# Experts' rows weighted and scattered with addition onto two sums per token while the experts run; the combine loads plain rows, and beta is added early

## The chip, the core and the metric

The kernel runs on one core of a Trainium2 chip. The metric is the device time in microseconds (us) of one launch, the median of several runs; the profile shows one execution.

## The reference

For 6250 tokens of 256 features: a layer norm, a graph sum over 100,000 edges and a second-order attention give a residual `x`. Then comes the part that the change touches, a mixture of 16 experts with the two best taken:

```python
z = layernorm(x)
logits = z @ gate_w + gate_b
vals, idx = top_k(logits, 2);  w = softmax(vals)
h = relu(einsum("bsh,ehf->bsef", z, w1) + b1)
expert_out = einsum("bsef,efh->bseh", h, w2) + b2
y = z + sum(w[..., None] * take(expert_out, idx))
out = x + layernorm(y) * gamma + beta
```

256 features, 512 hidden ones, all float32.

## The kernel before

Tokens are padded to 50 tiles of 128, worked in 10 units of 5 tiles. `acc` holds the residual of all of them in SBUF. After the edges and the attention come three stages.

**The gate**, unit by unit. DVE takes row statistics (`gate_front`, unit u + 1), ACT normalizes the five tiles into one of two buffers `zt5[k]` (`gate_z`, L896), PE turns them and forms logits, DVE takes the two best (`gate_back`), PE ranks them within their experts, and DVE writes the destination rows (`idxz`, L1448). POOL then scatters each of the five tiles twice into `z_dram` with indirect DMAs (`scatter_z`, L719), one for each expert chosen. `gate_z` waits until the scatters of the unit two before have read `zt5[k]`. At the end DVE works out from the counts which expert each of the 116 tiles of 128 slots belongs to and where it lies (L1550 to L1562), SP and ACT write a tile of zeros behind each expert's rows (L574, L915), and DVE works out where each token's two results will lie (L1568 to L1575) and the softmax (L1600 to L1605).

**The experts**, a loop over 116 tiles with four in its body. Each engine runs its own loop:

- PE, for tile t: `hidden(t+1)` (L1956, 8 matmuls, each of two passes), then waits for the slots of tile t+2, turns them (`turn_z(t+2)`, L1946 and L1947), then reads the expert's number and forms the outputs y(t) (L1976).
- ACT: ReLU of the hidden features (L934), then copies the turned slots out of PSUM (L921).
- DVE: adds b2 and writes `yo(t)` (L1592), then `copy_w(t+3)` copies the first weights of a later tile's expert (L1583).
- SP, for tile t: once tile t is turned, `load_z(t+4)` (L583) into one of four buffers `zt`; once `yo(t)` is there, its store to `y_dram` (L599) and `load_b2(t+2)` (L587). Each of these first reads a row or an expert number into a register.

**The combine**, unit by unit: POOL gathers 10 tiles of `y_dram` (L741), ACT normalizes the residual again (L943), DVE adds both weighted rows (L1466), takes statistics (L1021, L1025), ACT normalizes (L953), DVE multiplies by gamma (L1481), adds beta (L1486) and the residual (L1487), and SP stores 640 KB (L614).

Of the kernel before, what the change touches and what calls it, by code (L numbers as in the profile page):

```python
# [20 lines left out]
P = 128  # L21
# [44 lines left out]
R = NP + P  # L66
FT = 116
# [42 lines left out]
def program(nc, x, srcT, dstT, wT, wqkvT, bqkv, wprojT, bproj, temp, gate_w, gate_b, w1, b1T, w2, b2,  # L110
            gamma, beta, out):
    with ExitStack() as ctx:
# [21 lines left out]
        z_dram = nc.dram_tensor("z_dram", [ZR, C], F32).ap()  # L134
        y_dram = nc.dram_tensor("y_dram", [FT * P, C], F32).ap()

# [14 lines left out]
        topv = sb("topv", [P, NT, 2])  # L151
        posT = sb("posT", [P, NT, 2])
        expT = sb("expT", [P, NT, 2])
# [170 lines left out]
        mid = sb("mid", [P, 5120])  # L324
# [8 lines left out]
        zt5 = [mid[:, 2560 + 1280 * k:3840 + 1280 * k].rearrange("p (u c) -> p u c", u=U) for k in range(2)]  # L333
# [13 lines left out]
        zeros = mid[:, 2304:2304 + C]  # L347
# [9 lines left out]
        cmpy = mid[:, 3072:3072 + NT * 2 * X].rearrange("p (t e) -> p t e", e=X)  # L357
        cmpt = mid[0:1, 0:FTL * X].rearrange("p (t e) -> p t e", e=X)
        cmpc = mid[:, 0:X * NT].rearrange("p (e j) -> p e j", e=X)
        tau = mid[0:1, 1920:1920 + FTL]  # L360
        thr = mid[:, 2040:2040 + NT]
        etau = mid[0:1, 2096:2096 + FTL]
        rowI = late[0:1, 512:912][:, 0:FTL].bitcast(I32)
        expI = late[0:1, 512:912][:, FTL:2 * FTL].bitcast(I32)
        stau = late[0:1, 512:912][:, 2 * FTL:3 * FTL]
# [3 lines left out]
        yg = [big[:, 2560 * k:2560 * (k + 1)].rearrange("p (k u c) -> p k u c", k=2, u=U) for k in range(2)]  # L369
        zc = [big[:, 5120 + 1280 * k:6400 + 1280 * k].rearrange("p (u c) -> p u c", u=U) for k in range(2)]  # L370
        fc = [big[:, 7680 + 1280 * k:8960 + 1280 * k].rearrange("p (u c) -> p u c", u=U) for k in range(2)]
        fn = [big[:, a:a + U * C].rearrange("p (u c) -> p u c", u=U) for a in (10240, 12064)]
        gamma_b = big[:, 11520:11776]
        beta_b = big[:, 11776:12032]
        rc = big[:, 12048:12048 + U]
        nc5 = big[:, 12056:12056 + U]
# [49 lines left out]
        s_win = sems("s_win", 14)  # L426
# [4 lines left out]
        s_rg = sems("s_rg", NRB)  # L431
# [43 lines left out]
        s_w = sem("s_w")  # L475
        s_z = sem("s_z")
# [31 lines left out]
        NCONST = 26  # L508
# [9 lines left out]
        def _(sp):  # L518
# [1493 lines left out]
```

## Time and profile before

| | |
|---|---|
| median of 3 runs | 2754.63 us (2744.38 to 2778.39) |
| the profiled execution | 2739.31 us, its span 2737.4 us |
| granted TensorE clock, mean of the profiled span | 0.846 of full speed |
| PE / weight loads / DVE busy | 74% / 49% / 59% of the span |
| ACT / POOL busy | 30% / 47% |
| DMA | 243 MB, 89 GB/s on average |

Busy shares are averages over stages that are bound by different things. A stage has to be read by itself, from the timeline: which instruction waits last there, and for what. An engine's name with a q, as SPq, is its sequencer, and a DMA is listed there at its issue. Times "to landing" run from the issue to the semaphore.

### The profile page before, as it was taken

To read this page: it belongs to the slowest core of one execution; us is meant where nothing else is said; L and a number is where in the kernel's file an instruction comes from. 1 tells how busy PE (TensorE), PEld (TensorE's weight loads), DVE (VectorE), ACT (ScalarE), POOL (GpSimd) and SP (SyncE) were. 2 spreads that over 40 slices of the span, in tenths; PEclk is the share of its full clock that TensorE was granted. 3 is DMA by queue.
4 is the path that set the end of the run, shared out by engine and by line. 5 is a ranking of instruction groups with operands and counts; after the bars stand their busy time and mean duration, and the time that the engine had idled before them with its cause. 6 is when DMAs were issued, how large, how long until landed. Compare 5 with 4: busy or idle time off the path is not lost.

```text
span 2737.4 us, 43467 instructions
## 1 busy us (share of the span) xinstructions
PE 2028.5 (74%) x12138; PEld 1334.9 (49%) x12139; DVE 1622.2 (59%) x4163; ACT 819.7 (30%) x2169; POOL 1294.0 (47%) x1239
## 2 busy tenths in 40 slices
PE   4656766888888887888888888888552999999400
PEld 3434543455444453444444444444552999999300
DVE  6888888888888885444444445444444233233377
ACT  4645631111111111222222222222321444444332
POOL 1263343777777775565655566553454000000375
PEclk9768978999999998998989898988555999999755
DMA  5300010222222222232322222247822333333343
GB/s 168 119 31 27 24 28 28 83 81 81 79 80 81 81 82 64 83 89 81 89 77 83 84 89 86 84 76 65 296 73 98 99 106 106 104 105 108 100 120 119
DMA packets 147105, 243.46 MB, mean 89 GB/s; under 512 B 27874, under 2 KB 104932, under 8 KB 146949
## 3 DMA queue, kind: packets, MB, share of 16 engines
q0 software_dynamic: 55488, 149.11, 20.2%
q1 hardware_dynamic: 88500, 89.91, 10.2%
q10 hardware_dynamic: 2960, 2.55, 0.3%
q8 instruction: 75, 1.23, 0.2%
q14 instruction: 82, 0.66, 0.1%
HBM read 190.08 MB, written 51.38 MB: 88 GB/s over the span
## 4 chain that ended last, share of the span: by engine, by line
PE 36%; another core or an unknown queue 7%; issue 6%; DVE 5%; POOL 3%; DMA 2%; ACT 1%; DVEq 1%; SPq 1%; ACTq 0%; POOLq 0%
PE bank L1956 8%; PE b L1716 7%; PE bqk L1976 7%; PE bank L1833 4%; PE bqk L1844 3%; PE b L1728 2%; POOL big L741 2%; DMA big<-xn_dram,big 2%; POOL big L710 1%; PE bank L1916 1%; DVE big L1466 1%; DVE acc L1259 1%; ACT mid L896 1%; DVE big L1249 1%
## 5 line engine op out<-in xcount | busy, mean ns | idle before, releaser
L710 POOL DMA_INDIRECT big<-xn_dram,big x880 | 916.1, 1041 | 529.4 <-issue 201.4
L1716 PE MATMUL b<-big 128*128 128x256 f32 x1760 | 538.4, 434 | 96.8 <-DVE acc L1259 46.2
L1716 PEld LDWEIGHTS b<-big 128*128 128x128 f32 x1760 | 338.1, 210 | 340.2 <-issue 179.8
L1259 DVE TENSOR_TENSOR acc<-acc,b 128x256 f32 x440 | 183.9, 418 | 366.6 <-remote 195.0
L741 POOL DMA_INDIRECT big<-y_dram,idxz x100 | 112.3, 1123 | 491.6 <-issue 484.0
L1249 DVE TENSOR_SCALAR big<-big 128x128 f32<-128x128 f32 x880 | 300.5, 363 | 7.8 <-DVE big L1299 7.7
L879 ACT ACTIVATE big<-bank 128x512 f32<-128x512 f32 (+1 forms) x208 | 105.4, 576 | 501.9 <-PE bank L1833 276.9
L1956 PEld LDWEIGHTS bank<-late,mid 128*128 128x128 f32 x1872 | 228.6, 193 | 7.6 <-DVE mid L1583 1.7
L1956 PE MATMUL bank<-late,mid 128*128 128x128 f32 x1872 | 229.2, 276 | 1.5 <-DVE mid L1583 1.5
L1976 PE MATMUL bqk<-big,mid 128*128 x928 | 219.5, 379 | 0.0
L1592 DVE TENSOR_TENSOR mid<-bqk,mid 128x256 f32<-128x256 f32 x116 | 49.3, 425 | 246.4 <-PE bqk L1976 246.4
L1976 PEld LDWEIGHTS bqk<-big,mid 128*128 128x128 f32 x928 | 167.3, 190 | 17.9
L719 POOL DMA_INDIRECT z_dram<-mid,idxz x100 | 98.8, 988 | 120.9 <-DVE idxz L1448 91.6
L1766 PE MATMUL bqk<-big,mid 128*128 128x512 f32 (+1 forms) x392 | 144.4, 512 | 5.7 <-ACT mid L839 4.9
L1833 PE MATMUL bank<-big 32*128 32x512 f32 (+1 forms) x832 | 140.9, 672 | 9.7 <-ACT big L879 7.1
L934 ACT ACTIVATE mid<-bank,b1c 128x128 f32<-128x128 f32 x464 | 132.6, 368 | 51.6 <-issue 50.5
L846 ACT ACTIVATE big<-bqk 128x256 f32<-128x256 f32 x49 | 18.8, 384 | 369.9 <-DVE big L1296 354.9
L1279 DVE TENSOR_TENSOR big<-big 128x512 f32<-128x512 f32 x200 | 126.2, 685 | 0.0
L879 ACT ACTIVATE mid<-bank 128x512 f32<-128x512 f32 (+1 forms) x208 | 102.9, 582 | 70.8 <-PE bank L1833 53.1
L1279 DVE TENSOR_TENSOR mid<-big 128x512 f32<-128x512 f32 x192 | 121.4, 686 | 0.0
L1766 PEld LDWEIGHTS bqk<-big,mid 128*128 128x128 f32 x392 | 72.2, 194 | 99.4 <-issue 67.3
L674 POOL DMA_INDIRECT big<-sort_dram,idxg x49 | 54.2, 1106 | 138.4 <-DVEq L1116 109.4
(322 smaller groups left out, 3186.3 us busy)
## 6 DMA issues: line engine op xcount, KB each, us to landing
big<-w SPq DMA_DIRECT2D x8, 2048.0 KB
mid<-z_dram SPq DMA_DIRECT2D x120, 128.0 KB, 2.1
mid<-b SPq DMA_DIRECT2D x118, 128.0 KB, 3.0
y_dram<-mid SPq DMA_DIRECT2D x116, 128.0 KB, 1.7
big<-xn_dram,big POOLq DMA_INDIRECT x880
acc<-x_pad SPq DMA_DIRECT2D x10, 640.0 KB, 6.4
xn_dram<-big SPq DMA_DIRECT2D x10, 640.0 KB
y_out<-big SPq DMA_DIRECT2D x10, 640.0 KB
```

The source lines that it names most:

```text
L710: pool.indirect_dma_start(out=gx[t % EB], out_offset=None, in_=xn_dram, in_offset=bass.IndirectOffsetOnAxis(ap=dstA[:, t:t + 1], axis=0)). ...
L741: pool.indirect_dma_start(out=yg[k][:, m, j, :], out_offset=None, in_=y_dram, in_offset=bass.IndirectOffsetOnAxis(ap=idxz[k][:, j, m:m + 1 ...
L879: act.activation(feat[g % 2][h][:, 0:n], bank[h][:, 0:n], ACT.Square).then_inc(s_feat, 1)
L934: a = act.activation(hT[k % 2][:, c, :], ps_hT[k % 2][:, c * P:(c + 1) * P], ACT.Relu, bias=b1c[:, ds(ex * FC + c, 1)])
L1249: v.tensor_scalar(wd[t % (2 * EB)], iotaP, locA[:, t:t + 1], wA[:, t:t + 1], ALU.is_equal, ALU.mult).then_inc(s_d, 1)
L1259: v.tensor_tensor(mine, mine, ps_pair[p % 2][:, 0:C], ALU.add).then_inc(s_add, 1)
L1279: return v.tensor_tensor(kk[k][:, h], window(kd[k], h * DW, [[0, 16], [1, D]]), window(kd[k], h * DW + 1, [[1, 16], [1, D]]), ALU.mult)
L1716: a = pe.matmul(ps_pair[p % 2][:, 0:C], wd[t % (2 * EB)], gx[t % EB], start=(j == 0), stop=(j == 1))
L1766: a = pe.matmul(bqk[:, lo:hi], xT[s % 2][:, c, :], wqkv[:, c, lo:hi], start=(c == 0), stop=(c == 1))
L1833: pe.matmul(bank[h][:, 0:n], sel[D * h:D * (h + 1), g, :], qT[z % 2][D * h:D * (h + 1), 0:n], start=True, stop=True).then_inc(s_sel, 1)
L1956: a = pe.matmul(ps_hT[k % 2][:, f * P:(f + 1) * P], w1c[k % 2][:, c, f * P:(f + 1) * P], zT[k % 2][:, c, :], start=(c == 0), stop=(c == 1))
L1976: a = pe.matmul(ps_y2[k % 2], hT[k % 2][:, c, :], w2s[:, ds(ex, 1), c, :].rearrange("p o f -> p (o f)"), start=(c == 0), stop=(c == FC - 1))
```

## The change

`y_dram` and the gather from it go. Two sums per token take their place in DRAM, `sum_dram[0]` and `sum_dram[1]`. SP stores the gate's normalized rows into the first and zeros into the second. Rows of `z_dram` become 260 elements wide: behind a slot's 256 features lie its token's number, the first expert's number and the two softmax weights, which the gate now works out (`gate_exp` on ACT, six operations more on DVE). In the experts' loop DVE reads these four out of the slot tile (`meta`, three operations), ACT multiplies `yo` by the slot's weight (`weigh`), and POOL scatters the tile with addition onto `sum_dram[t % 2]`, each after the one two tiles before has landed. The slot buffers `zt` go from four to two, `yo` from two to four; `load_z(t+2)` waits for `meta(t)`. The combine loads both sums plainly (two transfers of 640 KB per unit), adds them, takes statistics, normalizes, multiplies by gamma on POOL and adds the residual, to which POOL has added beta during the experts' loop. The gate's loops and the combine's are written out. Rows that pad the slots are written in one transfer at the gate's end (they were zeros written at the start), and the zeros of `sum_dram[1]` at the start.

```diff
...
-        y_dram = nc.dram_tensor("y_dram", [FT * P, C], F32).ap()
+        z_dram = nc.dram_tensor("z_dram", [ZR, ZW], F32).ap()
+        sum_dram = [nc.dram_tensor(f"sum_dram{k}", [NP + P, C], F32).ap() for k in range(2)]
...
-        zt = [mid[:, 256 * k:256 * (k + 1)] for k in range(4)]
-        b2t = [mid[:, 1024 + 256 * k:1280 + 256 * k] for k in range(2)]
-        yo = [mid[:, 1536 + 256 * k:1792 + 256 * k] for k in range(2)]
-        w1c = [mid[:, 2048 + 1024 * k:3072 + 1024 * k].rearrange("p (c f) -> p c f", c=2) for k in range(2)]
-        hT = [mid[:, 4096 + 512 * k:4608 + 512 * k].rearrange("p (c n) -> p c n", c=FC) for k in range(2)]
+        padrow = mid[:, 2264:2264 + ZW]
+        zt = [mid[:, ZW * k:ZW * (k + 1)] for k in range(2)]
+        b2t = [mid[:, 520 + 256 * k:776 + 256 * k] for k in range(2)]
+        w1c = [mid[:, 1032 + 1024 * k:2056 + 1024 * k].rearrange("p (c f) -> p c f", c=2) for k in range(2)]
+        hT = [mid[:, 3080 + 512 * k:3592 + 512 * k].rearrange("p (c n) -> p c n", c=FC) for k in range(2)]
+        yo = [mid[:, 4104 + 256 * k:4360 + 256 * k] for k in range(4)]
...
-            for a in range(0, 20, U):
-                sp.dma_start(z_dram[X * R + a * P:X * R + (a + U) * P, :].rearrange("(p r) c -> p (r c)", p=P),
-                             zero).then_inc(s_zz, 16)
+            for a in range(0, NT, U):
+                sp.dma_start(sum_dram[1][a * P:(a + U) * P, :].rearrange("(p r) c -> p (r c)", p=P), zero).then_inc(s_zz, 16)
+            for k in range(2):
+                sp.dma_start(sum_dram[k][NP:NP + P, :], zero[:, 0:C]).then_inc(s_zz, 16)
+            sp.dma_start(beta_b[:], beta.partition_broadcast(P)).then_inc(s_gb, 16)
...
+            for u in range(NU):
+                sp.wait_ge(s_z, (u + 1) * U)
+                sp.dma_start(sum_dram[0][u * U * P:(u + 1) * U * P, :].rearrange("(u p) c -> p u c", p=P),
+                             zt5[u % 2][:, :, 0:C]).then_inc(s_zst[u % 2], 16)
+            sp.dma_start(z_dram[X * R:, :].rearrange("(r p) c -> p r c", p=P),
+                         padrow.unsqueeze(1).broadcast_to([P, 20, ZW])).then_inc(s_pz, 16)
...
-            for k in range(4):
+            for k in range(2):
                 load_z(k, k)
-            for k in range(2):
                 load_b2(k, k)
             with sp.Fori(0, FT // 4) as i:
                 for k in range(4):
                     t = 4 * i + k
                     sp.wait_ge(f_zT, t + 1)
-                    load_z(t + 4, k)
+                    sp.wait_ge(f_meta, t + 1)
+                    load_z(t + 2, k % 2)
                     sp.wait_ge(f_yo, t + 3)
-                    sp.dma_start(y_dram[ds(t * P, P), :], yo[k % 2]).then_inc(s_yst[k % 2], 16)
                     load_b2(t + 2, k % 2)
+            for k in range(2):
+                sp.wait_ge(s_ztin[k], 16 * (FT // 2 + 1))
+                sp.wait_ge(s_b2in[k], 16 * (FT // 2 + 1))
             for k in range(4):
-                sp.wait_ge(s_ztin[k], 16 * (FT // 4 + 1))
+                sp.wait_ge(s_ysc[k], 16 * (FT // 4))
+            sp.wait_ge(f_w, FT + 3)
             for k in range(2):
-                sp.wait_ge(s_yst[k], 16 * (FT // 2))
-                sp.wait_ge(s_b2in[k], 16 * (FT // 2 + 1))
...
+            for u in range(NU):
+                for k, a in ((0, zc[u]), (1, z1[u])):
+                    sp.dma_start(a, sum_dram[k][u * U * P:(u + 1) * U * P, :].rearrange("(u p) c -> p u c", p=P)).then_inc(s_zl[u // 2], 16)
+                if u == 0:
+                    sp.dma_start(gamma_b, gamma.partition_broadcast(P)).then_inc(s_gb, 16)
+            for u in range(NU):
+                sp.wait_ge(s_fo, u + 1)
+                sp.dma_start(out[u * U * P:(u + 1) * U * P, :].rearrange("(u p) c -> p u c", p=P), zc[u]).then_inc(s_ost, 16)
+            sp.wait_ge(s_ost, 16 * NU)
...
+            for t in range(FT):
+                pool.wait_ge(f_ys, t + 1)
+                if t >= 2:
+                    pool.wait_ge(s_ysc[(t - 2) % 4], 16 * ((t - 2) // 4 + 1))
+                pool.indirect_dma_start(out=sum_dram[t % 2], in_=yo[t % 4], in_offset=None,
+                                        out_offset=bass.IndirectOffsetOnAxis(ap=idxy[t % 4][:, 0:1], axis=0),
+                                        compute_op=ALU.add).then_inc(s_ysc[t % 4], 16)
+                if 4 <= t < 4 + NT:
+                    mine = acc[:, t - 4, :]
+                    pool.tensor_tensor(mine, mine, beta_b[:], ALU.add).then_inc(s_xb, 1)
+            pool.wait_ge(s_gb, 32)
+            for u in range(NU):
+                pool.wait_ge(s_fn, u + 1)
+                pool.tensor_tensor(zc[u], zc[u], gamma_b.unsqueeze(1).broadcast_to([P, U, C]), ALU.mult).then_inc(s_gm, 1)
...
+            def gate_exp(u):
+                act.wait_ge(s_df, u + 1)
+                act.activation(ew[:], df[:], ACT.Exp).then_inc(s_ew, 1)
...
+            for u in range(NU):
+                gate_root(u)
+                gate_z(u)
+                if u:
+                    gate_exp(u - 1)
+                gate_turn(u)
+            gate_exp(NU - 1)
...
+            def weigh(t, k):
+                act.wait_ge(f_yo, t + 3)
+                act.wait_ge(f_meta, t + 1)
+                act.activation(yo[k], yo[k], ACT.Copy, scale=wslot[k][:]).then_inc(f_ys, 1)
...
+            for t in range(1, 4):
+                expert(t, t)
+                weigh(t - 1, t - 1)
...
+                v.wait_ge(s_ew, u + 1)
+                link(v.tensor_scalar(wsum[:], ew[:], 1.0, None, ALU.add))
+                link(v.reciprocal(wsum[:], wsum[:]))
+                link(v.tensor_tensor(wlow[:], ew[:], wsum[:], ALU.mult))
+                mark(v.tensor_tensor(zt5[k][:, :, C + 2], wsum[:], wlow[:], ALU.subtract))
+                mark(v.tensor_copy(zt5[k][:, :, C + 3], wlow[:]))
...
+            def combine_front(u):
+
+                v.wait_ge(s_zl[u // 2], 64)
+                link(v.tensor_tensor(zc[u], zc[u], z1[u], ALU.add))
+                row_stats(lambda j: zc[u][:, j, :], mv[:, u * U:(u + 1) * U, :])
+                v.sem_inc(s_cst, 1)
+
+            def combine_out(u):
+
+                v.wait_ge(s_gm, u + 1)
+                v.tensor_tensor(zc[u], zc[u], acc[:, u * U:(u + 1) * U, :], ALU.add).then_inc(s_fo, 1)
...
+            def meta(t, k, i):
+
+                v.wait_ge(s_ztin[k % 2], 32 * i + 16 * (k // 2 + 1))
+                if not (isinstance(i, int) and i == 0):
+                    v.wait_ge(s_ysc[k], 16 * i)
+                mark(v.tensor_copy(idxy[k][:], zt[k % 2][:, C:C + 1]))
+                link(v.scalar_tensor_tensor(out=wmask[:], in0=zt[k % 2][:, C + 1:C + 2], scalar=etau[:, ds(t, 1)],
+                                            in1=zt[k % 2][:, C + 2:C + 3], op0=ALU.is_equal, op1=ALU.mult))
+                link(v.tensor_tensor(wslot[k][:], wmask[:], zt[k % 2][:, C + 3:C + 4], ALU.add))
+                v.sem_inc(f_meta, 1)
+
             def expert_four(i, first):
                 for k in range(4):
                     t = 4 * i + k
+                    meta(t, k, i)
                     v.wait_ge(f_y, t + 1)
                     v.wait_ge(s_b2in[k % 2], 32 * i + 16 * (k // 2 + 1))
-                    if not (first and k < 2):
-                        v.wait_ge(s_yst[k % 2], 32 * i + 16 * (k // 2))
-                    v.tensor_tensor(yo[k % 2], ps_y2[k % 2], b2t[k % 2], ALU.add).then_inc(f_yo, 1)
+                    v.tensor_tensor(yo[k], ps_y2[k % 2], b2t[k % 2], ALU.add).then_inc(f_yo, 1)
                     copy_w(t + 3, k + 1)
...
-                    pe.wait_ge(s_ztin[(k + 2) % 4], 16 * (i + 1 + (k + 2) // 4))
+                    pe.wait_ge(s_ztin[k % 2], 32 * i + 16 * (k // 2 + 2))
                     turn_z(t + 2, k + 2)
...
```

Beside this the windows of the edge sort and the record gather share semaphores in pairs.

## Rows read from the trace of the kernel before

**Rows 1.** The page: busy tenths of 40 slices, PE and the granted clock.

```profile
PE   4656766888888887888888888888552999999400
...
PEclk9768978999999998998989898988555999999755
```

**Rows 2.** Timeline (start us, us, engine, line): the first and last outputs.

```profile
2128.97 1.89 PE L1976 MATMUL bqk<-big,mid 128*128 x8
...
2558.11 1.89 PE L1976 MATMUL bqk<-big,mid 128*128 x8
```

**Rows 3.** Timeline of one tile of the experts' loop.

```profile
2300.62 1.89 PE L1976 MATMUL bqk<-big,mid 128*128 x8
...
2302.71 0.42 DVE L1592 TENSOR_TENSOR mid<-bqk,mid 128x256 f32<-128x256 f32 x1 [2.27 <-PE bqk L1976]
2303.31 0.35 SPq L599 DMA_DIRECT2D y_dram<-mid  x1
2303.64 0.69 DVE L1583 COPY mid<-big 128x1024 f32 x1 [0.50 <-issue]
...
2304.13 0.27 PE L1946 MATMUL b<-ident,mid 128*128 128x128 f32 x1
...
2304.35 1.89 PE L1976 MATMUL bqk<-big,mid 128*128 x8
2304.55 0.34 SPq L587 DMA_DIRECT2D mid<-b  x1
...
2305.87 0.35 SPq L583 DMA_DIRECT2D mid<-z_dram  x1
```

**Rows 4.** DMA issues: KB each, median us from issue to landing.

```profile
mid<-z_dram SPq DMA_DIRECT2D x120, 128.0 KB, 2.1
...
z_dram<-mid SPq DMA_DIRECT2D x4, 640.0 KB, 12.4
```

**Rows 5.** Timeline of the loop's start: the first slot loads and what they release.

```profile
2118.55 3.69 SPq L583 DMA_DIRECT2D mid<-z_dram  x4
...
2120.74 0.44 PE L1946 MATMUL b<-ident,mid 128*128 128x128 f32 x1 [25.20 <-DMA mid<-z_dram]
...
2122.83 1.28 ACT L926 ACT_TABLE_LOAD   x1
```

**Rows 6.** Timeline of the gate: a unit's last scatter and small operations of DVE.

```profile
2009.86 0.17 DVE L1448 CAST idxz<-posf 128x10 int32<-128x10 f32 x1 [0.32 <-DVE posf L1444]
...
2010.85 0.96 POOL L719 DMA_INDIRECT z_dram<-mid,idxz  x1 [11.87 <-DVE idxz L1448]
...
2022.23 0.96 POOL L719 DMA_INDIRECT z_dram<-mid,idxz  x1 [0.30 <-issue]
...
2024.02 0.24 DVE L1443 TENSOR_TENSOR late<-late 128x80 f32<-128x80 f32 x1
...
2024.86 0.60 ACT L896 ACTIVATE mid<-acc,nbias,rstd 128x256 f32 x1 [1.94 <-DMA z_dram<-mid,idxz]
```

**Rows 7.** Windows: PE, PEld, DVE, ACT, POOL busy us, PEclk, DMA share, GB/s.

```profile
1940.00:1945.00 5.00, 3.89 (x16) 3.10 (x16) 0.97 (x6) 1.20 (x2) 3.78 (x5) 0.50 1.07 377
2564.00:2565.00 1.00, 0.00 (x0) 0.00 (x0) 0.00 (x0) 1.00 (x3) 0.00 (x0) 1.00 0.12 28
2565.00:2566.00 1.00, 0.00 (x0) 0.00 (x0) 0.00 (x0) 1.00 (x3) 0.00 (x0) 0.53 0.04 12
```

**Rows 8.** Groups by line from 2560 us on: busy us, mean ns, idle before.

```profile
L741 POOL DMA_INDIRECT big<-y_dram,idxz x100 | 112.3, 1123 | 491.6 <-issue 484.0 <-DVE idxz L1471 7.7
...
L953 ACT ACTIVATE big<-big 128x256 f32<-128x256 f32 x50 | 25.7, 588 | 18.9 <-DVEq L1477 10.9 <-issue 8.0
...
L1021 DVE BATCH_NORM_STATS2 st<-big 128x6 f32<-128x256 f32 x50 | 17.3, 412 | 0.1
L1487 DVE TENSOR_TENSOR big<-big,acc 128x1280 f32<-128x1280 f32 x10 | 14.9, 1492 | 0.8 <-DVE big L1486 0.3
```

**Rows 9.** One line's instructions: the same POOL operation on 128x1280, ns min/median/max.

```profile
L682 POOL TENSOR_TENSOR acc<-acc,big x10: 2875/3067/4120, 127.9 to 156.0; 128x1280 f32<-128x1280 f32 x10
```

More of the change, by code:

```diff
@@ L66 @@
 R = NP + P
+ZW = C + 4
 FT = 116
@@ L721, in scatter_z @@
                                                 ).then_inc(s_zsc[k][j], 16)
-            pool.wait_ge(s_zz, 16 * 4)
-            with pool.Fori(0, NU // 2 - 1) as i:
-                for k in range(2):
-                    scatter_z(2 * i + k, k)
-            scatter_z(NU - 2, 0)
+            for u in range(NU - 1):
+                scatter_z(u, u % 2)
             pool.wait_ge(s_idxz, NU)
-            pool.memset(zeros, 0.0).then_inc(s_dz, 1)
+            pool.memset(padrow, 0.0).then_inc(s_dz, 1)
@@ L735, in _ @@
[L735 to L743 removed]
+            pool.wait_ge(s_gb, 16)
@@ L940, in combine_z, with combine_root, combine_rows @@
-            def combine_z(u, k):
+                    expert(t, k)
+                    weigh(t - 1, (k - 1) % 4)
+            weigh(FT - 1, (FT - 1) % 4)
+            def combine_root(u):
+                act.wait_ge(s_cst, u + 1)
+                act.activation(std5[:], mv[:, u * U:(u + 1) * U, 1:2].rearrange("p u o -> p (u o)"), ACT.Sqrt, bias=eps[:]
+                               ).then_inc(s_crt, 1)
+            def combine_rows(u):
+                act.wait_ge(s_csc, u + 1)
                 for j in range(U):
@@ L972, in _ @@
+                a.then_inc(s_fn, 1)
+            for u in range(NU):
+                combine_root(u)
+                combine_rows(u)
         @block.vector
@@ L1536, in _ @@
             gate_front(0)
-            unit_scales(0, NU + NK)
-            gate_pair(0, True)
-            loop(1, NU // 2 - 1, gate_pair)
-            gate_pair(NU // 2 - 1, False)
+            scales(0, s_grt, s_gsc)
+            for u in range(NU):
+                if u < NU - 1:
+                    gate_front(u + 1)
+                gate_back(u)
             join()
@@ L1609, in _ @@
             loop(1, FT // 4, expert_four)
-            for k in range(2):
-                v.tensor_copy(idxz[k][:], posT[:, k * U:(k + 1) * U, :]).then_inc(s_idxc, 1)
-            v.sem_inc(s_ask, 1)
-            v.wait_ge(s_gb, 32)
-            combine_front(0, 0, 0)
-            combine_scales(0)
-            combine_pair(0, True)
-            loop(1, NU // 2 - 2, combine_pair)
-            combine_pair(NU // 2 - 2, False)
-            combine_pair(NU // 2 - 1, False, last=True)
+            v.wait_ge(s_xb, NT)
+            for u in range(NU + 2):
+                if u < NU:
+                    combine_front(u)
+                if u >= 2:
+                    combine_out(u - 2)
+                if u < NU:
+                    scales(u, s_crt, s_csc)
         @block.tensor
@@ L1933, in _ @@
             logits(0, 0)
-            with pe.Fori(0, NU // 2 - 1) as i:
-                for k in range(2):
-                    rank(2 * i + k)
-                    logits(2 * i + k + 1, 1 - k)
-            rank(NU - 2)
-            logits(NU - 1, 1)
-            rank(NU - 1)
+            for u in range(NU):
+                rank(u)
+                if u < NU - 1:
+                    logits(u + 1, (u + 1) % 2)
             pe.wait_ge(s_cc, NU + 1)
```

326 lines of the change are left out of this document (126 added, 200 removed).

## The prediction

> **What bounds the kernel now.** I read the page's slices first [rows 1]. PE is 80 to 90% busy through the edges and the attention, drops to 5, 5, 2 tenths in the gate, stands at 9 in the experts' loop and at 0 in the combine. The change leaves the first 1900 us alone but for some zero writes, so three stages count: gate, experts, combine. Next the timeline of each.
>
> The experts' loop is bound by PE. Its outputs y(t) start every (2558.11 − 2128.97) / 115 = 3.73 us [rows 2], and one tile's rows show PE going from y to hidden to turn to the next y with no gap, while DVE waits 2.27 us for PE [rows 3]. 116 × 3.73 = 433 us. Every transfer has slack there: slots are loaded four tiles ahead.
>
> The gate's ends are the scatters: ten in a row, one every (2022.23 − 2010.85) / 9 = 1.26 us, and POOL idle between units, 11.87 us at most [rows 6]. The combine begins where the last y ends, 2558.11 + 1.89 = 2560.0, and takes 2737.4 − 2560.0 = 177.4 us. POOL is busy for 112.3 us of it with 100 gathers [rows 8], and with the 0.3 us of issue beside each they set the pace.
>
> **The experts' loop after the change.** This is where I expect the loss. Two things are new around `load_z`: there are two slot buffers, so tile t+2 goes into the one of tile t, and the load waits for `meta(t)`, since meta reads the last four columns of that buffer. Now put meta into DVE's order: yo(t−1), `copy_w(t+2)`, `meta(t)`. And the load into PE's order: y(t−1), hidden(t+1), **wait for slots t+2**, turn, y(t). So each y(t) needs a load that can't be issued before y(t−1) has ended and DVE has worked off three things. The loop becomes a ring through four engines, and its period is the sum around it:
>
> - y end to the end of yo: 2300.62 + 1.89 = 2302.51 to 2303.13, 0.62 us [rows 3].
> - to the end of the weight copy: 2304.33, another 1.20 us, 0.50 of it reading the expert's number into a register [rows 3].
> - meta: three operations on one column, 0.17 us each by the smallest shown [rows 6], and waits against register values around them. Below: 3 × 0.17 with small gaps, 0.6 us. Above: each gap as long as the 0.50 us of the same engine in the loop [rows 3], 1.5 us. I take 0.9.
> - SP reads the row number and issues: four such loads take 3.69 us, of which the last one's issue is 0.34 as in a load_b2; (3.69 − 0.34) / 3 − 0.34 = 0.78 us of preparation [rows 3, 5], and 0.18 us from yo's end to the store waiting on it shows the signal [rows 3]. 0.9 us; bounds 0.7 and 1.2 (the 0.98 us between L587's end and L583, and the signal) [rows 3].
> - issue to PE: 2120.74 − 2118.55 = 2.19 us [rows 5]; the median landing is 2.1 [rows 4]. Bounds 1.9 and 2.6, the latter for the scatters now running beside it.
> - turn to the start of y: 4.35 − 4.13 = 0.22 us [rows 3]. PE's sequencer then reads the expert's number. Before, it ran ahead of the array; now it has just been stopped, and the read shows. By DVE's 0.50 us for the same read, less the turning beside it: 0.3, bounds 0 and 0.5 [rows 3].
> - y itself: 1.89 us [rows 3].
>
> Sum 0.62 + 1.20 + 0.90 + 0.90 + 2.19 + 0.22 + 0.30 + 1.89 = 8.22 us. hidden (under 2 us) lies inside the wait, so PE stands idle for some 4 us per tile. The granted clock holds for about that long: after the last y at 2560.0 it was 1.00 until 2565 and 0.53 in the microsecond after [rows 7], so it may fall in some gaps. A turning matmul of the loop's cold start took 0.44 us against 0.27 [rows 3, 5], and a y at half clock 1.9 us more. I take a quarter of that, 0.5 us per tile: 8.72. The loop takes 116 × 8.72 = 1012 us, **+579**.
>
> The Trainium skill ("Trainium Kernel Development and Optimization", Best Practices) says to double-buffer so that transfers and compute overlap. It speaks for the change: two buffers would be enough and the loop would stay at 3.73 us. What speaks against it here are the rows: the buffer is given back so late in the ring that both buffers' lead is used up before the load starts.
>
> What else is new in the loop lies beside this. weigh is one more ACT operation of the size of L896, 0.60 us at most [rows 6], per tile, on an engine that would be busy for a quarter of the period. The scatter is issued by POOL in 0.96 us [rows 6]; each waits for the one two tiles before, and the meta of tile t for the scatter of t−4. No row prices a scatter that adds. From below it is the plain scatter, 2.63 us from issue to the next user (2022.23 to 2024.86) [rows 6]; it would have to take over 14 us, nearly two periods, to be felt. The nearest row is the plain one, so I take nothing. Had the loop kept 3.73 us, 6 us would be the limit. Beta on POOL, 50 times a fifth of a 128x1280 operation, 0.6 us each [rows 9], is hidden by POOL's waits, as is the lost y store. By the skill ("DMA: Bandwidth & Descriptors", Anatomy of one DMA) a transfer by POOL costs 2.0 us plus bytes over 436 GB/s, an estimate of 2.3 us for 131 KB; it prices no addition, and the sum is the same.
>
> **The gate.** ACT's order is now root(u+1), z(u+1), exp(u), and z(u+1) waits for the scatters of unit u−1. DVE needs exp(u) before `idxz(u)`, so scatter(u) starts only when scatter(u−1) has landed. From a unit's first scatter: 11.38 to its last, 2.63 to z, 0.60 for z, 1.28 for a table load [rows 5, 6] and some 0.25 for the exp, then DVE's five small operations and the ranks' six, 2.8 us at 0.17 to 0.24 each with gaps, and 1.0 from idxz to POOL (2009.86 to 2010.85) [rows 6]: 19.9 us per unit. Now it is about 18: L719 fills 12.6 and POOL waits for the rest. +2 us on eight units, less what writing out the loops saves: +10, bounds 0 and +20. The end of the gate loses DVE's three large operations and gains one write of 2560 rows (2.7 MB); four transfers that write 640 KB each to the same tensor land 12.4 us after their issue [rows 4], which is about as long as the zero tiles behind the experts take beside it. I take nothing; it is in the +20. The zeros for `sum_dram[1]`, 6.5 MB at the start, run before the first sorted chunk is stored.
>
> **The combine.** The gathers go. From the last y: yo 0.62, weigh about 1.0, the scatter 0.96 + 2.63 [rows 3, 6], then loads of 13.1 MB. In the gate the weights arrive at 377 GB/s [rows 7]; at that rate a unit's 1.3 MB take 3.5 us, and DVE needs more: two adds of 1.49, statistics 17.3 / 10 = 1.73, and 1.3 for the rest, 6.0 us [rows 8]. So DVE is the bound: 5.2 + 2.2 + 7 with the signals about 15 to the first sum, since a pair of units shares its wait; 60 for ten units; and behind the last ACT 25.7 / 10 = 2.6 and a root 0.3, POOL's gamma 3.07 [rows 8, 9], an add 1.49, and a store that I take at 4, twice a slot load [rows 4], with the signals 13: 88 us in place of 177.4, **−89**. Bounds −105 and −65, the last if loads pace it.
>
> **Sum.** Against the profiled execution's 2739.3 us: + 579 + 10 − 89 = 3239 us. The median of the runs lies 15 us above that execution, which I leave inside the range. Forecast **3240**.
>
> **Rivals.**
> - *The load stays hidden.* If two buffers are enough, the loop stays near 3.73 us, and the combine's gain shows: 2739 + 10 − 89 = 2660, faster. It decides below a period of 3.73 + 79 / 116 = 4.4 us. The ring's two certain parts alone, a load of 2.19 and y of 1.89, give 4.1, and DVE's yo and copy 1.8 more, so only a misread order could bring it. 7 in 100.
> - *The clock stays at half.* y takes 1.9 us more and the turning 0.3 in every tile: period 10.4, 2739 + 10 + 774 − 89 = 3434. For it speaks a gap of 4 us per tile; against it that y and hidden, 1.9 us each at full clock, would follow each other for over 7 us at half clock with no gap, and that the loop's start, as cold [rows 5], was followed by 3.73 us per tile throughout [rows 2, 3]. 11 in 100.
> - *The addition is slow.* A scatter-add of 24 us gives a period of 12: 2739 + 10 + 959 − 89 = 3619. Only the lack of a row speaks for it. 4 in 100.
> - *The ring as forecast*, period 7.2 to 9.6: 78 in 100.
>
> **How the numbers follow.** The ring from its low ends is 0.62 + 1.2 + 0.6 + 0.7 + 1.9 + 0.22 + 0 + 1.89 = 7.1, with 7.2 for a little clock: 2739 + 0 + 403 − 105 = 3037. The upper end takes in the half-clock rival: 2739 + 10 + 774 − 80 = 3443. So 3035 to 3445. Slower by over 2% (about what a measurement can tell) in all cases but the first: 0.92. Faster 0.06. Within 2%, 0.02, a period between 4.0 and 4.9, which nothing points to.
>
> **What would show it.** In the profile after, y's starts 8 to 9 us apart; PE waiting for the slot load (L583's successor) in each tile, before the turn; SP issuing that load right behind DVE's meta; DVE idle for y as before; POOL idle for most of the loop. The granted clock in the loop below 1.00 if the 0.5 us is right. The combine some 90 us with DVE busy throughout, and unit starts in the gate 20 us apart. Wrong if PE waits for the scatter or the loop's period is under 5 us.

## The result and the profile after

The changed kernel takes 3382.9 us (median of four runs, 3377.6 to 3402.15), the kernel before 2762.4 us over its four runs (2744.38 to 2778.39). The ratio is 1.226, 95% interval 1.218 to 1.234: slower by 22.6%, some 620 us. The forecast was 3240 us, with a range of 3035 to 3445.

| stage, in the profiled executions | before | after | difference | forecast |
|---|---|---|---|---|
| to the gate's first scatter | 1933.2 | 1975.2 | +42.0 | 0 |
| gate, first to last scatter | 177.3 | 203.9 | +26.6 | +10 |
| last scatter to first y | 18.5 | 20.4 | +1.9 | 0 |
| experts, first y to last matmul of y | 430.6 | 1100.4 | +669.8 | +579 |
| from there to the end | 177.8 | 100.5 | −77.3 | −89 |
| span | 2737.4 | 3400.4 | +663.0 | +500 |

The first row can't be laid to the change. Nearly all code up to there is the same but for the zero writes and the shared semaphores, and the edge gathers begin at 471.2 and 470.2 us. The profiled execution of the kernel before was quicker than all four of its runs (2739 us, median 2762), that of the changed kernel the longest of its own (3402, median 3383). In the study's other profiles the first scatter starts between 1945.0 and 1973.4 us, at 1961.6 in the one whose code there is that of before (before_two_slots); 1933.2 and 1975.2 are the two ends of all twelve. Without this row 621 us are left, as the medians differ.

The page of the changed kernel, busy tenths and granted clock, to be held against [rows 1]:

```profile
PE   5477678888887788878878844366666666666650
...
PEclk8788789999998888889888855587888777777875
```

PE stands at 6 in the experts' loop where it stood at 9, and the clock mostly at 7 and 8 where it was 9. The same shows in a window of the loop (PE, PEld, DVE, ACT, POOL busy, PEclk, DMA share, GB/s):

```profile
2300.00:2500.00 200.00, 128.60 (x546) 105.71 (x546) 31.25 (x105) 40.38 (x126) 48.60 (x42) 0.78 0.22 41
```

One tile of the loop in the timeline, beside [rows 3]:

```profile
2502.21 3.44 PE L1976 MATMUL bqk<-big,mid 128*128 x8 [0.67 <-issue]
...
2505.68 0.42 DVE L1599 TENSOR_TENSOR mid<-bqk,mid 128x256 f32<-128x256 f32 x1 [7.79 <-PE bqk L1976]
2506.61 0.69 DVE L1580 COPY mid<-big 128x1024 f32 x1 [0.50 <-issue]
2506.94 0.34 SPq L612 DMA_DIRECT2D mid<-b  x1
...
2507.52 0.16 DVE L1590 TENSOR_TENSOR wslot<-wmask,mid 128x1 f32<-128x1 f32 x1
2508.62 0.34 SPq L608 DMA_DIRECT2D mid<-z_dram  x1
...
2510.76 0.44 PE L1946 MATMUL b<-ident,mid 128*128 128x128 f32 x2 [3.33 <-DMA mid<-z_dram]
...
2511.73 3.54 PE L1976 MATMUL bqk<-big,mid 128*128 x8 [0.53 <-issue]
```

The ring, the closed chain of waits from one y to the next, is there. y ends at 2505.65; yo, the weight copy and meta follow on DVE to 2507.68; SP issues the slot load at 2508.62; PE, idle for 3.33 us before it turns the slots, names that load as what it waited for, and starts the next y at 2511.73. Grouped by line over the loop (busy us, mean ns, idle before and what ended it):

```profile
L1976 PE MATMUL bqk<-big,mid 128*128 x839 | 355.0, 597 | 49.8 <-issue 49.8
...
L1946 PE MATMUL b<-ident,mid 128*128 128x128 f32 x208 | 54.8, 353 | 309.1 <-DMA mid<-z_dram 309.1
```

The first of these rows in the kernel before:

```profile
L1976 PE MATMUL bqk<-big,mid 128*128 x856 | 202.5, 379 | 0.0
```

Each pass of y lasts 597 ns on average where it lasted 379, and 309 us of PE's idle time end with the slot load, 309.1 / 104 = 2.97 us per tile. Where the clock stood is told by windows over the parts of the tile shown: y, hidden, the wait, the turn with the register read, the next y.

```profile
2502.21:2505.65 3.44, 3.44 (x10) 2.85 (x11) 0.00 (x0) 1.29 (x5) 2.31 (x2) 0.57 0.29 33
2505.65:2507.43 1.78, 1.78 (x16) 1.59 (x15) 1.25 (x4) 0.00 (x0) 0.00 (x0) 1.00 0.08 10
2507.43:2510.76 3.33, 0.01 (x1) 0.01 (x1) 0.22 (x2) 0.00 (x0) 0.00 (x0) 1.00 0.28 79
2510.76:2511.73 0.97, 0.44 (x3) 0.21 (x3) 0.00 (x0) 0.50 (x2) 0.00 (x0) 1.00 0.00 0
2511.73:2515.27 3.54, 3.54 (x9) 2.85 (x10) 0.00 (x0) 1.42 (x5) 2.31 (x2) 0.54 0.28 31
```

The granted clock is full (2.4 GHz) in hidden, through the whole wait and in the turn, and at half (1.2 GHz) for nearly all of both y. In the gate, the units' scatters start 19.3 us apart (2034.03, 2053.33), but for the first distance, 39.5 us, and the last, 17.5:

```profile
2007.40 2.57 ACT L932 ACTIVATE mid<-acc,nbias,rstd 128x256 f32<-128x256 f32 x5 [29.25 <-DMA sum_dram<-mid]
...
2014.74 0.97 POOL L744 DMA_INDIRECT z_dram<-mid,idxz  x1 [27.00 <-DVE idxz L1501]
...
2034.03 0.97 POOL L744 DMA_INDIRECT z_dram<-mid,idxz  x1 [6.85 <-DVE idxz L1501]
...
2053.33 0.97 POOL L744 DMA_INDIRECT z_dram<-mid,idxz  x1 [6.86 <-DVE idxz L1501]
```

ACT waited 29.25 us for the store of an earlier unit into `sum_dram[0]`, which SP had queued behind 16.8 MB of weights: the loads go out from 1952.75 us on, the first store at 1993.74.

### The profile page after: what moved, and what is told of

Its sections match the earlier page's. It is cut to its first block, busy times and chain, and to the rows that moved or that the text cites. A ratio compares the mean times of both kernels' runs of the same rounds, so it can differ in the third digit from the quotient of the medians.

```text
span 3400.4 us, 43794 instructions
## 1 busy us (share of the span) xinstructions
PE 2308.4 (68%) x12138; PEld 1518.1 (45%) x12139; DVE 1622.8 (48%) x4451; ACT 862.5 (25%) x2260; POOL 1440.9 (42%) x1317
## 4 chain that ended last, share of the span: by engine, by line
PE 29%; DMA 9%; issue 9%; another core or an unknown queue 7%; DVE 6%; SPq 4%; DVEq 3%; POOL 3%; ACT 1%; POOLq 0%; ACTq 0%
PE bqk L1976 12%; DMA mid<-z_dram 7%; PE b L1718 6%; PE bank L1835 3%; PE bqk L1846 2%; PE b L1730 2%; PE b L1946 2%; POOL z_dram L744 2%; SPq L607 2%; DVEq L1577 2%; DMA big<-xn_dram,big 1%; SPq L586 1%; POOL big L735 1%; PE bqk L1882 1%
## 5 line engine op out<-in xcount | busy, mean ns | idle before, releaser
L735 POOL DMA_INDIRECT big<-xn_dram,big x880 | 926.6, 1053 | 559.9 <-PE b L1718 237.3
L765 POOL DMA_INDIRECT sum_dram<-mid,idxy x116 | 180.3, 1554 | 905.3 <-ACT mid L967 905.3
L1976 PE MATMUL bqk<-big,mid 128*128 x928 | 392.0, 596 | 56.0 <-issue 56.0
L1976 PEld LDWEIGHTS bqk<-big,mid 128*128 128x128 f32 x928 | 265.3, 299 | 143.9 <-issue 89.9
L1946 PE MATMUL b<-ident,mid 128*128 128x128 f32 x236 | 62.1, 353 | 372.3 <-DMA mid<-z_dram 372.3
L1956 PEld LDWEIGHTS bank<-late,mid 128*128 128x128 f32 x1872 | 291.6, 236 | 16.6
L1956 PE MATMUL bank<-late,mid 128*128 128x128 f32 x1872 | 279.3, 313 | 0.0
L962 ACT ACTIVATE late<-b 128x256 f32<-128x256 f32 x118 | 45.3, 384 | 901.9 <-PE b L1946 901.9
L1946 PEld LDWEIGHTS b<-ident,mid 128*128 128x128 f32 x236 | 27.0, 160 | 394.8 <-DMA mid<-z_dram 367.9
```

The source lines that it names most:

```text
L735: pool.indirect_dma_start(out=gx[t % EB], out_offset=None, in_=xn_dram, in_offset=bass.IndirectOffsetOnAxis(ap=dstA[:, t:t + 1], axis=0)). ...
L765: pool.indirect_dma_start(out=sum_dram[t % 2], in_=yo[t % 4], in_offset=None, out_offset=bass.IndirectOffsetOnAxis(ap=idxy[t % 4][:, 0:1], ...
L1946: a = pe.transpose(ps_zT[k % 2][:, P * c:P * (c + 1)], zt[k % 2][:, P * c:P * (c + 1)], ident[:])
L1956: a = pe.matmul(ps_hT[k % 2][:, f * P:(f + 1) * P], w1c[k % 2][:, c, f * P:(f + 1) * P], zT[k % 2][:, c, :], start=(c == 0), stop=(c == 1))
L1976: a = pe.matmul(ps_y2[k % 2], hT[k % 2][:, c, :], w2s[:, ds(ex, 1), c, :].rearrange("p o f -> p (o f)"), start=(c == 0), stop=(c == FC - 1))
```

## The experiments

All of them start from the changed kernel unless said otherwise. Starts and stage lengths are read as in the table above. A period is the loop's length divided by its 116 tiles; from start to start of y it is up to 0.1 us more (9.55 us in the changed kernel, whose period is 9.49). Where a mean over 111 tiles is given, it is taken from the starts and ends of the instructions in the trace, without the loop's ends.

### Four slot buffers

```diff
...
-        zt = [mid[:, ZW * k:ZW * (k + 1)] for k in range(2)]
+        zt = [mid[:, ZW * k:ZW * (k + 1)] for k in range(4)]
...
-                    load_z(t + 2, k % 2)
+                    load_z(t + 4, k)
...
```

To make room, two of the four `yo` lie in tensors that are free by then (`upper` and `ones`; `mv`, `rstd`, `nbias` and scratch). The waits on the slot loads follow the four buffers.

> The changed kernel with four slot buffers instead of two, load_z(t+4) instead of load_z(t+2); everything else kept (four yo, the wait for meta, the scatter with addition). Theory, the ring through one load: the load has three tiles more of lead, PE no longer waits for it, y starts every 3.7 to 3.8 us again (9.6 now), the loop takes about 435 us in place of 1101, so about 3383 - 666 = 2717 us, range 2690 to 2760: the gain of the combine minus the gate's loss shows. Rival, the scatter with addition sets the pace once the loop is fast: a period of 5 us or more, with POOL or DVE's meta waiting for a scatter, 2860 us or more. Rival, the wait for meta costs even with four buffers: period 5 to 6, PE waiting for the slot load.

Measured: 2718.2 us, ratio to the kernel before 0.984 (0.977 to 0.992). The loop takes 430.7 us, y starts every 3.73 us, the gate 203.8 and the end 100.4 us as in the changed kernel.

```profile
2401.13 1.89 PE L1978 MATMUL bqk<-big,mid 128*128 x8
...
2402.38 1.55 POOL L767 DMA_INDIRECT sum_dram<-mid,idxy  x1 [2.00 <-ACT mid L969]
2402.39 0.34 SPq L608 DMA_DIRECT2D mid<-z_dram  x1
...
2404.86 1.89 PE L1978 MATMUL bqk<-big,mid 128*128 x8
```

```profile
2300.00:2500.00 200.00, 200.00 (x1393) 188.86 (x1393) 91.10 (x269) 102.97 (x323) 106.40 (x80) 1.00 0.59 106
```

The whole loss is in the lead of one load, that is, in how long before its use it is issued. With four buffers PE is busy for all of the 200 us of the window, so the wait for meta costs nothing, and the clock is 1.00. The scatter with addition sets no pace either: POOL waited for an earlier one to land 12 times in 116 (25.4 us in all), and no other engine waited for a scatter.

### The kernel before with two slot buffers

```diff
-                    load_z(t + 4, k)
+                    load_z(t + 2, k % 2)
```

> The kernel before with one thing of the change: two slot buffers, load_z(t+2). There is no meta; the load waits only for the turned tile and for its place in SP's queue, behind the wait for yo(t-1), its store and load_b2. Theory: two buffers alone make a ring. yo 0.62, signal and store 0.53, load_b2 with its preparation 1.24, preparation of the load 0.98, landing 2.19, the turn and the register read 0.97 as in the changed kernel, y 1.89 to 3.5: 8.4 to 10 us per tile, 3300 to 3490 us in all. Rival, only the wait for meta does the harm and two buffers are enough without it: period 3.73, 2762 us as before.

Measured: 3505.5 us, ratio 1.272 (1.261 to 1.283); period 10.1 us, both just above what was expected. So the two buffers do the harm by themselves. Without meta the load still stands in SP's queue behind the wait for yo, its store and load_b2:

```profile
2510.79 0.42 DVE L1592 TENSOR_TENSOR mid<-bqk,mid 128x256 f32<-128x256 f32 x1 [8.48 <-PE bqk L1976]
2511.42 0.36 SPq L599 DMA_DIRECT2D y_dram<-mid  x1
...
2512.77 0.35 SPq L587 DMA_DIRECT2D mid<-b  x1
2514.46 0.34 SPq L583 DMA_DIRECT2D mid<-z_dram  x1
...
2516.49 0.48 PE L1946 MATMUL b<-ident,mid 128*128 128x128 f32 x1 [3.33 <-DMA mid<-z_dram]
...
2517.59 3.78 PE L1976 MATMUL bqk<-big,mid 128*128 x8 [0.41 <-issue]
```

The load is issued 3.25 us behind the end of yo (2511.21 to 2514.46), later than in the changed kernel (2506.10 to 2508.62, 2.52 us), where no store stands before it. The means over 111 tiles are 2.76 and 2.59 us, and y lasts 3.64 us against 3.39.

### Shortening the ring: meta ahead of the weight copy

```diff
...
-                    meta(t, k, i)
+                    if first and k == 0:
+                        meta(t, k, i)
...
                     v.tensor_tensor(yo[k], ps_y2[k % 2], b2t[k % 2], ALU.add).then_inc(f_yo, 1)
+                    if k < 3:
+                        meta(t + 1, k + 1, i)
+                    elif not last:
+                        meta(t + 1, 0, i + 1)
                     copy_w(t + 3, k + 1)
...
```

> The changed kernel, two slot buffers, with DVE's meta(t+1) moved ahead of copy_w(t+3). Theory: the weight copy's 0.50 + 0.69 = 1.2 us leave the ring, the period goes from 9.6 to about 8.4, about 3383 - 140 = 3243 us; a shorter gap of PE may also keep the clock up and give more, down to 3150. Rival, the load doesn't wait for DVE but for SP's own queue: then at most 0.5 us per tile, 3325 us or more.

Measured: 3364.4 us, 18.5 less than the changed kernel; period 9.26 where 9.49 was. The theory's number was wrong and the rival's right:

```profile
2508.43 0.42 DVE L1600 TENSOR_TENSOR mid<-bqk,mid 128x256 f32<-128x256 f32 x1 [6.38 <-PE bqk L1982]
...
2509.08 0.16 DVE L1590 TENSOR_TENSOR wslot<-wmask,mid 128x1 f32<-128x1 f32 x1
2509.72 0.34 SPq L612 DMA_DIRECT2D mid<-b  x1
...
2511.09 0.34 SPq L608 DMA_DIRECT2D mid<-z_dram  x1
...
2513.21 0.69 PE L1952 MATMUL b<-ident,mid 128*128 128x128 f32 x2 [2.59 <-DMA mid<-z_dram]
```

Meta now ends at 2509.24, but SP had turned to load_b2 first, and the slot load follows it by 1.37 us. From yo's end (2508.85) to the load it is 2.24 us, 0.28 less than before the edit (2.26 and 2.59 us in the means). 0.28 × 116 = 32 us by the ring; 26 us of the loop's length were measured.

### The same, with the slot load ahead of load_b2

```diff
...
                     load_z(t + 2, k % 2)
-                    sp.wait_ge(f_yo, t + 3)
-                    load_b2(t + 2, k % 2)
+                    sp.wait_ge(f_yo, t + 2)
+                    load_b2(t + 1, (k + 1) % 2)
...
```

> meta_first (3364 us) with SP's order turned: load_z(t+2) goes out before load_b2, which is moved a tile back. Theory, in meta_first the slot load stood behind load_b2 in SP's queue (issued 1.37 us behind it), which ate the 1.2 us gained on DVE: now the load is issued some 0.7 us earlier, period 9.26 to 8.5, about 3364 - 80 = 3284 us, range 3220 to 3310. Rival, SP's order doesn't matter: 3364 us.

Measured: 3147.4 us, 217 less than meta_first where 80 were expected. The direction was right, the size not: in the tile shown the load goes out 1.59 us behind yo's end, 0.65 us earlier, and the period fell by 1.89 us (7.37).

```profile
2500.92 1.99 PE L1983 MATMUL bqk<-big,mid 128*128 x8 [0.53 <-issue]
...
2502.95 0.42 DVE L1601 TENSOR_TENSOR mid<-bqk,mid 128x256 f32<-128x256 f32 x1 [4.33 <-PE bqk L1983]
...
2504.96 0.34 SPq L608 DMA_DIRECT2D mid<-z_dram  x1
...
2507.11 0.44 PE L1953 MATMUL b<-ident,mid 128*128 128x128 f32 x2 [2.41 <-DMA mid<-z_dram]
...
2508.09 1.99 PE L1983 MATMUL bqk<-big,mid 128*128 x8 [0.54 <-issue]
```

y lasts 1.99 us in this tile. Over 2300 to 2900 us its mean is 198.6 / 80 = 2.48 us, against 218.6 / 65 = 3.36 us in meta_first, and the granted clock from 2300 to 2500 us was 0.87 where it was 0.77. The means over 111 tiles split the gain: yo's end to the load 2.26 us in meta_first and 1.42 here, 0.84 less; issue to the turn 2.17 and 2.09; y 3.39 and 2.41, 0.98 less; from the turn to y 1.01 us in both. A shorter ring shortens PE's gap (2.41 us before the turn here), and the clock gives back somewhat more than the edit itself.

### Keeping PE busy in the gap

```diff
...
                     hidden(t + 1, k + 1)
+                    for q in range(6):
+                        pe.matmul(bank[q % 2][:, 0:C], ident[:], w2s[:, 0, q % FC, :], start=True, stop=True)
```

> The changed kernel, two slot buffers, with six idle matmuls of 128x256 (0.47 us each at full clock, 2.8 us) behind hidden(t+1), into banks that nobody reads, so that PE stays busy while it waits for the slot load. They leave nothing out and change no result. Theory, the clock falls in the gap and makes y last 3.4 us instead of 1.9 and the turn longer: with the gap filled the clock is 1.00, the period falls from 9.5 to about 8.0 us, the whole to about 3383 - 174 = 3209 us, range 3180 to 3250. Rival, the clock has nothing to do with the gap: y stays at 3.4 us and the time at 3383 or above.

Measured: 3238.9 us, 144 less than the changed kernel, from work that does nothing.

```profile
2300.00:2500.00 200.00, 167.16 (x915) 139.84 (x914) 35.64 (x120) 46.16 (x144) 55.56 (x48) 0.98 0.26 48
```

```profile
2500.82 1.99 PE L1978 MATMUL bqk<-big,mid 128*128 x8 [0.53 <-issue]
...
2504.43 2.76 PE L1971 MATMUL bank<-big,ident 128*128 128x256 f32 x12
...
2505.80 0.34 SPq L608 DMA_DIRECT2D mid<-z_dram  x1
...
2507.89 0.44 PE L1946 MATMUL b<-ident,mid 128*128 128x128 f32 x2 [0.71 <-DMA mid<-z_dram]
...
2508.86 1.99 PE L1978 MATMUL bqk<-big,mid 128*128 x8 [0.53 <-issue]
```

The clock is 0.98, y lasts 1.99 us, the period is 8.18 us. The load goes out and lands as before (2.61 and 2.11 us in the means, 2.59 and 2.11 without the filler), so the difference, 9.49 − 8.18 = 1.31 us per tile or 152 us, is the price of the clock; the ring at nearly full clock is 8.2 us.

### The exp in the gate

```diff
                 gate_root(u)
-                gate_z(u)
                 if u:
                     gate_exp(u - 1)
+                gate_z(u)
```

> The changed kernel with ACT's exp of unit u-1 moved ahead of the normalizing of unit u in the gate. Theory: a unit's scatters no longer wait for those of the unit before to land; the distance between units falls from 19.3 us to between 13 and 17.7 us, the gate's scatters from 204 us to 177 us or less, the whole to 3340 to 3365 us, with the experts' loop unchanged at 1100 us. Rival, the gate is bound by something else (the logits' chain of the next unit): distance stays at 18 to 19 us, no change.

A single run, 3374.1 us, above the 3340 to 3365 expected. It alone would tell little, but the stage does: the gate's scatters take 177.5 us in place of 203.9, the loop 1100.8 as before, and the first scatter starts within 2 us of the profile compared with (1973.4 and 1975.2), which took 3402.15 us. The wait of exp for the scatters of the unit before was worth 26 us.

### Four slot buffers, without the addition

This one starts from the kernel with four slot buffers. It leaves the addition out, so each sum holds only the row that was written last.

```diff
...
-                                        out_offset=bass.IndirectOffsetOnAxis(ap=idxy[t % 4][:, 0:1], axis=0),
-                                        compute_op=ALU.add).then_inc(s_ysc[t % 4], 16)
+                                        out_offset=bass.IndirectOffsetOnAxis(ap=idxy[t % 4][:, 0:1], axis=0)).then_inc(s_ysc[t % 4], 16)
...
```

> four_slots with a plain scatter in place of the one with addition; the sums then hold only the row written last, which leaves the addition out of the result. It prices the addition: POOL took 1.55 us to issue a scatter with addition and it landed 3.8 us later. Expected without: 0.96 us and about 2.6 us, and the same total of 2718 us, because at 3.73 us per tile neither is waited for much. Rival, the addition costs time in the loop: 10 us or more less.

A single run, 2706.9 us. The loop takes 430.6 us, as with the addition (430.7); of the 14.4 us between the two profiled executions (2721.3 and 2706.9) 14.0 lie ahead of the gate's first scatter (1969.7 and 1955.7 us), in unchanged code. POOL's issue takes 0.96 us in place of 1.55, the landing 2.6 us in place of 3.8. So adding costs 0.6 us of POOL and 1.2 us of landing per tile of 128 rows, off the path at either pace.

### Four slots with three more edits, then the weight loads and gamma

Four slots, exp before z, the combine's statistics without their copy, and the first unit of the combine waiting for its own loads alone:

> Four slot buffers as in four_slots (2718 us), and three things more: exp before the normalizing in the gate (26 us less in exp_before_z), the combine's statistics written straight into mv without the copy that took 1.79 us beside POOL's multiplication and 0.17 alone (about 1.6 us of each unit, 14 us in all if DVE is the bound there), and the first unit of the combine waiting for its own two loads alone and not for those of two units (about 5 us). Expected 2718 - 26 - 14 - 5 = 2673 us, range 2650 to 2695, 3% faster than the kernel before. Rival, the combine is paced by its transfers and not by DVE: then the last two bring nothing, 2692 us.

Measured: 2685.0 us, ratio 0.973 (0.969 to 0.978). The gate's scatters take 178.6 us, 25 less than in four_slots. The end takes 95.3 us in place of 100.4. No run parts the two edits there, but the trace does: the first sum starts 12.5 us behind the last matmul of y in place of 18.1, and once the loads are in, a unit takes 7.20 us in place of 7.52, so leaving out the copy brought 0.3 us per unit and not the 1.6 expected. In the changed kernel each copy but the first lasted 1.8 us beside POOL's multiplication, which is how long POOL still ran:

```profile
3321.93 0.17 DVE L1063 COPY mv<-mv 128x10 f32<-128x10 f32 x1
...
3332.06 2.88 POOL L774 TENSOR_TENSOR big<-big 128x1280 f32<-128x1280 f32 x1 [3.51 <-ACT big L1000]
...
3333.18 1.79 DVE L1063 COPY mv<-mv 128x10 f32<-128x10 f32 x1
```

```profile
L1518 DVE TENSOR_TENSOR big<-big,acc 128x1280 f32<-128x1280 f32 x10 | 25.2, 2518 | 5.4 <-POOL big L776 4.2
```

The copy starts at 3333.18 and ends at 3334.97 with POOL's operation (3332.06 + 2.88 = 3334.94); alone it took 0.17. Without it the wait moved to the next two-input operation: the residual add now lasts 2.52 us on average, mostly 3.0, and 1.49 before [rows 8].

Then the weight loads were spread over the gate, one behind each unit's store:

```diff
...
-            for e in range(0, X, 4):
-                sp.dma_start(w1s[:, e:e + 4], w1[e:e + 4].rearrange("e (c p) f -> p e c f", p=P)).then_inc(s_w, 16)
-            for e in range(0, X, 4):
-                sp.dma_start(w2s[:, e:e + 4], w2[e:e + 4].rearrange("e (c p) f -> p e c f", p=P)).then_inc(s_w, 16)
...
                              zt5[u % 2][:, :, 0:C]).then_inc(s_zst[u % 2], 16)
+                if u < 8:
+                    e = 4 * (u % 4)
+                    ws, wd_ = (w1s, w1) if u < 4 else (w2s, w2)
+                    sp.dma_start(ws[:, e:e + 4], wd_[e:e + 4].rearrange("e (c p) f -> p e c f", p=P)).then_inc(s_w, 16)
...
```

> best (2685 us) with SP's eight weight loads of 2 MB spread over the gate, one behind each of the first eight stores of a unit into sum_dram[0], in place of all eight ahead of them. Theory: in the changed kernel one unit's normalizing waited 29 us for such a store, which stood behind 16.8 MB of weights in SP's queue (31.9 us in best); with the loads spread this wait goes and the gate's scatters take 178.6 - 25 = 153 us or less, the whole about 2660 us. Rival, the weights' traffic slows the scatters wherever it lies: the wait is spread too and nothing is gained, 2685 us.

Measured: 2658.8 us, ratio 0.963 (0.955 to 0.970). The gate's scatters take 164.7 us, 14 less than in best and not 25: the 31.9 us wait for the store is gone, but POOL's longest wait between two units is still 13.4 us, where it was 28.7, and there are others of 1.9 to 6.2. 26 us less by the medians, of which only the 14 can be laid to the edit.

Last, gamma back on DVE:

> best_spread with gamma's multiplication of the combine on DVE in place of POOL. Theory: POOL's operation of 2.88 us keeps DVE's copy or two-input add waiting until it ends (2.52 us a residual add in best, 1.49 us in the kernel before), so DVE pays 1.8 us per unit for POOL's help; with gamma on DVE its adds last 1.49 again, the multiplication costs 1.49, and a unit takes 7.0 us and not 7.4, the last unit's way is 1.4 us shorter: about 5 us less than best_spread. Rival, the residual add is slow for another reason (its own operands): adds stay at 2.5 us, about 15 us more than best_spread.

Measured: 2658.4 us, ratio 0.964 (0.956 to 0.972), no difference from best_spread; neither the 5 us less nor the rival's 15 us more came. The adds last 1.49 us again (14.9 us for ten), so the cause of the 2.52 us is shown; the multiplication's own 1.49 us eats what they give back (a unit takes 7.22 us in place of 7.20), and the end takes 93.0 us in place of 92.7.

Which engine is held up depends on which started first. In best POOL's multiplication began 0.02 us ahead of DVE's sum, in best_spread 0.03 us behind it; the rows of best, then of best_spread:

```profile
2604.13 2.88 POOL L776 TENSOR_TENSOR big<-big 128x1280 f32<-128x1280 f32 x1 [2.69 <-ACT big L1002]
2604.15 4.20 DVE L1511 TENSOR_TENSOR big<-big 128x1280 f32<-128x1280 f32 x1 [2.70 <-DMA big<-sum_dram]
```

```profile
2586.53 1.49 DVE L1511 TENSOR_TENSOR big<-big 128x1280 f32<-128x1280 f32 x1 [2.64 <-DMA big<-sum_dram]
2586.56 4.20 POOL L776 TENSOR_TENSOR big<-big 128x1280 f32<-128x1280 f32 x1 [2.69 <-ACT big L1002]
```

## Why the prediction was right, and where its numbers were off

**The mechanism** was right in place and cause. The ring's terms, as forecast and as one tile of the changed kernel shows them (2505.65 to 2515.27):

| term | forecast | measured |
|---|---|---|
| y end to yo end | 0.62 | 0.45 |
| to the end of the weight copy | 1.20 | 1.20 |
| meta | 0.90 | 0.38 |
| to the load's issue | 0.90 | 0.94 |
| issue to PE | 2.19 | 2.14 |
| turn and register read | 0.52 | 0.97 |
| y | 1.89 + 0.5 for the clock | 3.54 |
| sum | 8.72 | 9.62 |

**The term that failed** is the clock. I took "a quarter" of y's 1.9 us for a gap of some 4 us, which was 2.97. The mean y over the loop lasted 392.0 / 116 = 3.38 us, so it paid 1.49 us and not 0.5, four fifths of the full price. The period, 9.49 us, came out between the forecast's 8.72 and the half-clock rival's 10.4, just inside the 7.2 to 9.6 given to the ring as forecast. The filler run prices the clock's whole effect on the period at 1.31 us, 152 us of the launch. The argument that PE's long busy stretch at half clock would bring the clock back was true, and useless: it came back with the end of y, in time for hidden, which nobody waits for. Nor was the fear that the clock "may fall in some gaps" the right picture. In the tile shown it stayed full through the whole gap and the turn and fell 0.3 us into y. Over 113 tiles of the trace half clock fills 0.08 us of a mean gap of 2.97, 2.93 of y's 3.39 and 0.91 of hidden's 2.39; 86 gaps are at full clock throughout, and 3 y. So the engine's few microseconds of idle time were paid for afterwards, by the work behind them, which here is the part of the ring that everybody waits for. At a clock of 0.98 the filler's ring was 8.18 us against my 8.22 without the clock.

**Meta** was 0.5 us shorter and **the turn with the register read** 0.45 us longer than taken; that they cancel is luck. The clock has no part in the latter: from the turn to y it is 0.97 us in the filler's tile too (2507.89 to 2508.86), and in the mean 1.01 us in the changed kernel and 1.00 with the filler. The forecast's 0.22 us was the distance between two starts while y followed without a stop. Here the register read lies between them, so the turn's whole 0.44 us counts, and the read shows as 0.53 us of issue before y.

**The scatter with addition** was taken as a plain one of 2.63 us. It lands in 3.8 us, and both limits (14 us here, 6 us at the fast pace) are far off.

**The gate** cost 26.6 us and not 10. The distance of 19.3 us between units was forecast at 19.9. What I missed is SP's queue: the new stores into `sum_dram[0]` stand behind the weight loads, and `gate_z` waits for them. I had costed the store at nothing without asking what lay ahead of it in its queue. The experiments price the parts: exp's place costs 26 us (203.9 to 177.5) and the store's wait 14 (178.6 to 164.7). With both mended the gate's scatters take 164.7 us, 9 to 13 less than the gate of the kernel before (173.9 in before_two_slots, 177.3), where I had taken some 6 for the loops that are written out; what else makes this up was not tested.

**The combine** gave 77 us and not 89. A unit takes 7.5 us of DVE and not 6.0, of which the copy has 1.8 while it waits out POOL's multiplication, which I had costed as free help; the first sum came later behind the last y's end (3300.5 to 3318.05, 17.5 us), not 15.

**The sum** was 143 us short of the median (3382.9 − 3240): 91 us in the loop, 17 in the gate, 12 in the combine, 2 between, and the 23 us by which the profiled execution of before was quicker than the median of its four runs (145, with rounding and the runs' spread).

The rival that the load stays hidden, which the Trainium skill's rule on double buffers ("Trainium Kernel Development and Optimization", Best Practices) spoke for, is refuted by both kernels with two slots: 1100 and 1172 us for the loop against 431.

## What to carry to other kernels

A buffer count is a lead, not a number of overlapping stages. Ask at what point of the loop the buffer is given back and what stands in the issuing queue between that and the load; if the answer lies behind this iteration's last result, two buffers make a ring through every engine, and its period is the sum around it. When PE's wait grows to some 3 us in a tile, as here, price its clock too, and put the price on the work that follows the gap. A new DMA in a queue can inherit what was queued ahead of it, and a new wait on it passes this on (here 29 us of ACT, 14 us of the gate).

## What the runs showed of the hardware

- With PE idle for 2.97 us on average ahead of the turn in each tile of 9.5 us, y was at half clock for 2.93 of its 3.39 us, while the gap itself was nearly all at full clock. With 2.04 us of idle time (meta_first_load_first) y took 2.41 us, and 0.84 us off the load's issue saved 1.89 us per tile. Idle matmuls in the gap raised the granted clock from 0.78 to 0.98 and made the kernel 144 us faster.
- POOL's `tensor_tensor` on 128x1280 (2.88 us) holds up DVE's copies and two-input adds until it ends (0.17 us became 1.8, 1.49 became 3.0 or 4.2), but not DVE's statistics: in best five `bn_stats` (from 2598.14 us) beside POOL's operation (2598.55 to 2601.43) took 1.73 us as alone. With DVE 0.03 us ahead it is POOL that took 4.20 us. The Trainium skill ("SBUF — State Buffer", Terms) describes a port pair that DVE and GpSimd lock against each other for a full instruction. The runs agree for copy and add, either way round; they show that not every DVE operation is held up.
- An indirect scatter of 128 rows of 1 KB takes POOL 0.96 us plain and 1.55 us with float32 addition, and lands in 2.6 and 3.8 us.
- Reading a register on PE just after a wait showed as 0.53 us ahead of y; in the kernel before, where PE doesn't wait there, y has no idle time before it.
